# Four graph layers on one core: the last layer's sum over heads in halves and partly on TensorE, and a weight-turning stage folded into the next

## The reference

```python
# third layer, after attention: enc is [2048, 512]
out = relu(enc @ W1.T + b1)      # W1 256x512
out = relu(out @ W2.T + b2)      # W2 128x256
out = relu(out @ W3.T + b3)      # W3 256x128
out = out @ W4.T + b4            # W4 512x256
# fourth layer, 8 heads of 64, 10000 pairs (sub, obj) among the first 1500 rows
q = inst[sub] @ Wq.T + bq;  k = inst[obj] @ Wk.T + bk
scores = zeros(8, n, n).at[:, sub, obj].set((q * k).sum(-1) / 8)
scores = where(mask, -inf, scores); diagonal set to 1e-7
attn = softmax(scores, axis=2)
return (attn.sum(axis=0) / 8) @ inst
```

## Time and profile before

| | |
|---|---|
| median of 3 runs | 4013.73 us (4013.5 to 4014.74) |
| the profiled execution | 4014.29 us, span 4012.5 us |
| busy over the span | PE 3447.6 us (86%), DVE 3285.9 (82%), ACT 2812.9 (70%), POOL 1317.8 (33%) |
| mean granted clock of PE | 0.922 |
| relation stage, first `peaks` to last `finish` | 3316.42 to 4006.81 us |
| its busy times | DVE 631.3 us, PE 612.4, ACT 330.2 |

### The profile page before, as it was taken

The page is one execution under the profiler, slowest core; times in us unless marked ns, Lnnn a source line. Parts: engine busy times, 40 slices in busy tenths (PEclk is TensorE's granted clock), DMA queues, the critical chain, the costliest instruction groups (busy, mean ns, idle before and its releaser), DMA issues. The chain is left out here.

```text
span 4012.5 us, 55910 instructions
## 1 busy us (share of the span) xinstructions
PE 3447.6 (86%) x20136; PEld 2041.2 (51%) x20136; DVE 3285.9 (82%) x5486; ACT 2812.9 (70%) x3711; POOL 1317.8 (33%) x1035
## 2 busy tenths in 40 slices
PE   7899999879899744889999848999997997989898
PEld 4799999434444322444444414378775443333333
DVE  4799998579999798599999875399996408999997
ACT  5799998459899998399989971377784325444443
POOL 0476443014445355044445342056550200000000
PEclk9999999889999876999999969999998998989989
DMA  7711110311111020311111005210001211111110
GB/s 242 261 45 34 30 34 13 98 45 50 51 42 45 25 76 28 109 48 37 32 40 40 14 6 181 115 23 22 20 21 48 75 41 58 48 45 40 53 37 16
DMA packets 167767, 229.14 MB, mean 57 GB/s; under 512 B 90578, under 2 KB 101744, under 8 KB 164240
## 3 DMA queue, kind: packets, MB, share of 16 engines
q1 hardware_dynamic: 148592, 182.94, 14.5%
q0 software_dynamic: 18896, 42.46, 3.3%
HBM read 150.19 MB, written 74.89 MB: 56 GB/s over the span
## 5 line engine op out<-in xcount | busy, mean ns | idle before, releaser
L1736 DVE SCALAR_TENSOR_TENSOR junk<-expd,mid 128x2048 bf16<-128x2048 f32 x440 | 1034.8, 2352 | 14.1
L594 ACT ACTIVATE steepz<-s1b,thr_h 128x512 bf16<-128x512 f32 (+1 forms) x928 | 774.3, 916 | 32.0 <-DVE A L665 20.8
L1624 ACT ACTIVATE junk_s<-expd,nmid 128x2048 bf16<-128x2048 f32 x244 | 486.5, 1994 | 5.3 <-POOL nmid L1690 2.7
L1627 ACT ACTIVATE junk_s<-expd,nmid 128x2048 bf16<-128x2048 f32 x244 | 486.6, 1994 | 0.0
L748 PE MATMUL acc<-V,B 128*128 128x198 bf16 x4096 | 443.1, 251 | 34.2 <-DVE B L667 13.6
L755 PE MATMUL acc<-V,adjT 128*128 128x99 bf16 (+1 forms) x5248 | 417.0, 218 | 0.3 <-issue 0.3
L2217 PE MATMUL psS<-KT,qs 64*128 64x512 f32 x1024 | 333.0, 684 | 74.3 <-DVE m L2318 69.5
L1688 POOL TENSOR_SCALAR reach<-above,lack 128x1 f32<-128x1 f32 x196 | 203.2, 1037 | 579.6 <-ACT lack L1635 579.2
L1690 POOL TENSOR_SCALAR nmid<-reach,steps,nmid 128x1 f32<-128x1 f32 x196 | 357.7, 1825 | 20.6
L755 PEld LDWEIGHTS acc<-V,adjT 128*128 128x128 bf16 x5248 | 341.1, 98 | 40.6 <-issue 1.4
L748 PEld LDWEIGHTS acc<-V,B 128*128 128x128 bf16 x4096 | 342.1, 99 | 38.0 <-issue 23.8
(11 more groups left out here) (309 smaller groups left out, 6433.7 us busy)
## 6 DMA issues: line engine op xcount, KB each, us to landing
rows<-in_adj_dram SPq DMA_DIRECT2D x16, 1024.0 KB, 8.7
s1b<-sT_dram SPq DMA_DIRECT2D x32, 512.0 KB
block<-adj_dram SPq DMA_DIRECT2D x32, 512.0 KB, 4.4
plain_table<-rows POOLq DMA_DIRECT2D x16, 512.0 KB, 8.0
adj_dram<-adjT POOLq DMA_DIRECT2D x4, 2048.0 KB, 21.2
veil_table<-fill POOLq DMA_DIRECT2D x64, 128.0 KB
y_dram<-yo SPq DMA_DIRECT2D x32, 256.0 KB, 2.0
step_dram<-xo SPq DMA_DIRECT2D x32, 256.0 KB, 2.0
```

Of the source, the lines that this page charges most:

```text
L594: act.activation(steepz[:, m % RELUS, :], s1b[:, q % 4, :], ACT.Relu, bias=thr_h[:, u, 1, j:j + 1], scale=STEEP).then_inc(relu_ready, 1)
L1624: act.activation(junk_s[:, 0, :], expd[:, slot[i], :], ACT.Relu, bias=col(nmid, i), accum_out=col(above, i)).then_inc(sums_ready, 1)
L1627: act.activation(junk_s[:, 1, :], expd[:, slot[i], :], ACT.Sign, bias=col(nmid, i), accum_out=col(signs, i)).then_inc(sums_ready, 1)
L1736: link(dve.scalar_tensor_tensor(junk[:, :], e, col(mid, i), e, ALU.is_gt, ALU.mult, accum_out=found))
```

## The change

In the perceptron, `weight_transpose_stage` is gone. Its four loads stand at the head of SP's program in the real stage, and its twenty turns are packed in six units (4, 4, 2, 2, 4 and 4 blocks), one behind each of the first six tiles on PE, each with one ACT copy, through the buffer `psN` that `weights` uses too. ACT's wait for the biases moves from the head of its program to iteration 6.

In the relation layer (names as above):

- Of the eight heads, 0 to 4 go through DVE's sum. Head 5 is the buffer that they are summed into; `attn` is gone. Heads 6 and 7 are only scaled, on ACT (`scale`, 2048 columns each), and PE adds the three parts while it turns them: each block of `psT` is three accumulating turns in place of one, 48 per tile in place of 16.
- The sum on DVE is cut in halves of 1024 columns: 12 instructions per tile in place of 8 of 2048, halves in alternation, so that each needs the one before the last.
- G grows from 10 slots to 8 short-lived and 6 long-lived; `attnT` shrinks to three groups; the output row is written over the input row.
- All orders are new. An iteration has eight steps n. PE: n=0 S0 A7 (of tile t-3); n=1 S1 T0; n=2 S2 T1 A0 A1; n=3 S3 T2 A2; n=4 S4 T3 A3; n=5 S5 A4; n=6 S6 A5; n=7 S7 A6. DVE, with W a half-width sum: n=0 P0, W11 and diagonal of tile t-2, finish of t-3; n=1 P1, weights, W0, W1; n=2 to 4 P and two W; n=5 to 7 P and one W.

```diff
--- before.py
+++ after.py
...
-    def weight_transpose_stage(self, items):
...
-            def _(pe):
-                for i, (n, r, c) in enumerate(blocks):
-                    pe.wait_ge(w_in[n], 16)
-                    if i >= 4:
-                        pe.wait_ge(t_copied, i - 3)
-                    pe.transpose(psT[:, i % 4, 0:P], loads[n][:, r, tile(c)], self.ident[:, :]).then_inc(t_ready, 1)
...
-            def _(act):
-                for i, (n, r, c) in enumerate(blocks):
-                    act.wait_ge(t_ready, i + 1)
-                    act.copy(items[n][1][:, c, tile(r)], psT[:, i % 4, 0:P]).then_inc(t_copied, 1)
...
-            self.weight_transpose_stage([(a["L2_gnn_W1"], w1t), (a["L2_gnn_W2"], w2t),
-                                         (a["L2_gnn_W3"], w3t), (a["L2_gnn_W4"], w4t)])
+            raw = [self.sb(st, "raw", [P, w.shape[0] // P, w.shape[1]])
+                   for w in (a[f"L2_gnn_W{i}"] for i in (1, 2, 3, 4))]
...
+            units = [(0, [(r, k) for k in range(KD)], w1t[:, :, tile(r)]) for r in range(E1)]
+            units += [(1, [(0, c) for c in range(E1)], w2t[:, :, :]),
+                      (2, [(r, 0) for r in range(E3)], w3t[:, 0, :].rearrange("p (r i) -> p r i", r=E3))]
+            units += [(3, [(r, c) for r in range(KD)], w4t[:, c, :].rearrange("p (r i) -> p r i", r=KD)) for c in range(E3)]
...
+                for i in range(4):
+                    sp.dma_start(raw[i][:, :, :], a[f"L2_gnn_W{i + 1}"].rearrange("(r p) c -> p r c", p=P)
+                                 ).then_inc(raw_in[i], 16)
...
+                def small_weights(n):
+                    _, blocks, dst = units[n]
+                    act.wait_ge(wt_ready, n + 1)
+                    act.copy(dst, psN[:, n % 2, 0:len(blocks), :]).then_inc(wt_copied, 1)
...
-                act.wait_ge(b_in, 64)
                 for t in range(NT + 1):
                     if t < NT:
                         exps(t)
+                    if 1 <= t <= UNITS:
+                        small_weights(t - 1)
                     if t >= 9:
                         weights(t - 9)
+                    if t == 6:
+                        act.wait_ge(b_in, 64)
...
+                def small_weights(n):
+                    i, blocks, _ = units[n]
+                    pe.wait_ge(raw_in[i], 16)
+                    if n >= 2:
+                        pe.wait_ge(wt_copied, n - 1)
+                    for k, (r, c) in enumerate(blocks):
+                        mm = pe.transpose(psN[:, n % 2, k, :], raw[i][:, r, tile(c)], self.ident[:, :])
+                    mm.then_inc(wt_ready, 1)
...
                     self.transpose_tiles(pe, psT, t, nat, t_ready, t_copied)
+                    if t < UNITS:
+                        small_weights(t)
...
-        SLOTS = 10
+        SCALED = 2
+        SUM = H - SCALED - 1
+        HEADS_DONE = 2 * (SUM + 1)
+        SUMMED = HEADS_DONE + 1
+        LONG = SCALED + 1
+        SHORTS, LONGS = 8, 6
+        TURNED = 3
...
-            Gb = self.sb(st, "Gb", [P, SLOTS - H // 2, N])
...
-            attn = self.sb(st, "attn", [P, 2, N])
-            attnT = self.sb(st, "attnT", [P, NT, P])
+            attnT = self.sb(st, "attnT", [P, TURNED, 4, P])
...
-                return Ga[:, n, :] if n < H // 2 else Gb[:, n - H // 2, :]
+                return slot((t * SUM + h) % SHORTS if h < SUM else SHORTS + (t * LONG + h - SUM) % LONGS)
+
+            def parts(t):
+                return [G(t, h) for h in range(SUM, H)]
...
-                            sp.wait_ge(weighed, (H + 1) * (t - 2) + 1)
+                            sp.wait_ge(weighed, SUMMED * (t - 2) + 4)
...
-                            sp.wait_ge(xo_ready, t - 3)
+                            sp.wait_ge(x_out[t % 2], 16 * (t // 2 - 1))
...
-                        pe.wait_ge(weighed, (H + 1) * (t + 1))
+                        pe.wait_ge(weighed, SUMMED * (t + 1))
+                        pe.wait_ge(scaled, SCALED * (t + 1))
                     if t >= 1 or gp >= 1:
                         pe.wait_ge(t_copied, 4 * t + gp)
                     for j in range(4):
-                        mm = pe.transpose(psT[:, j, :], attn[:, t % 2, tile(4 * gp + j)], self.ident[:, :])
+                        for n, part in enumerate(parts(t)):
+                            mm = pe.matmul(psT[:, j, :], part[:, tile(4 * gp + j)], self.ident[:, :],
+                                           start=(n == 0), stop=(n == SCALED), is_transpose=True)
...
-                    if gp == 3 and half == 1:
+                        mm = pe.matmul(psO[:, :], attnT[:, (4 * t + gp) % TURNED, j % 4, :], nat[:, j, :], start=(j == 0), stop=(j == NT - 1))
+                    if half == 1:
                         mm.then_inc(o_ready, 1)
 
+                turned = {1: (0,), 2: (1,), 3: (2,), 4: (3,)}
+                applied = {2: (0, 1), 3: (2,), 4: (3,), 5: (4,), 6: (5,), 7: (6,)}
                 for t in range(NT + 2):
                     if t < NT:
                         pe.wait_ge(q_in[t % 2], 16 * (t // 2 + 1))
-                    for m in range(PAIRS):
+                    for n in range(2 * PAIRS):
                         if t < NT:
-                            scores(t, m, 0)
+                            scores(t, n // 2, n % 2)
+                        if n == 0 and t >= 3:
+                            apply(t - 3, 3, 1)
                         if t >= 2:
-                            transposes(t - 2, m)
-                        if t >= 2 and m >= 1:
-                            apply(t - 2, m - 1, 0)
-                        if t < NT:
-                            scores(t, m, 1)
-                        if t >= 2 and m >= 1:
-                            apply(t - 2, m - 1, 1)
-                    if t >= 2:
-                        apply(t - 2, 3, 0)
-                        apply(t - 2, 3, 1)
+                            for gp in turned.get(n, ()):
+                                transposes(t - 2, gp)
+                            for part in applied.get(n, ()):
+                                apply(t - 2, part // 2, part % 2)
+                apply(NT - 1, 3, 1)
...
-                    if t >= 1 and gp == 0:
-                        act.wait_ge(o_ready, t)
-                    act.copy(attnT[:, 4 * gp:4 * gp + 4, :], psT[:, :, :]).then_inc(t_copied, 1)
+                    if 4 * t + gp >= TURNED:
+                        act.wait_ge(o_ready, 4 * t + gp - TURNED + 1)
+                    act.copy(attnT[:, (4 * t + gp) % TURNED, :, :], psT[:, :, :]).then_inc(t_copied, 1)
...
+                def exps(t, h):
+                    act.wait_ge(scores_read, unit(t, h // 2, 1, h % 2) + 1)
...
+                def scale(t, h):
+                    act.wait_ge(r_ready, t + 1)
+                    act.activation(G(t, h), G(t, h), ACT.Copy, scale=r[:, h:h + 1]).then_inc(scaled, 1)
 
...
+                    if t >= 2:
+                        copies(t - 2, 0)
+                    if t < NT:
+                        exps(t, 0)
+                        exps(t, 1)
+                    if t >= 2:
+                        copies(t - 2, 1)
+                    if 1 <= t <= NT:
+                        scale(t - 1, SUM + 1)
+                    if t >= 2:
+                        copies(t - 2, 2)
+                    if t < NT:
+                        exps(t, 2)
+                        exps(t, 3)
+                    if t >= 2:
+                        copies(t - 2, 3)
+                    if t < NT:
+                        exps(t, 4)
+                        exps(t, 5)
+                        count(t)
+                    if 1 <= t <= NT:
+                        scale(t - 1, SUM + 2)
+                    if t < NT:
+                        exps(t, 6)
+                        exps(t, 7)
...
+                        if t * SUM + h >= SHORTS:
+                            before = t * SUM + h - SHORTS
+                            dve.wait_ge(weighed, SUMMED * (before // SUM) + 2 * order.index(before % SUM) + 2)
+                    elif t * LONG + h - SUM >= LONGS:
+                        dve.wait_ge(t_ready, 4 * ((t * LONG + h - SUM - LONGS) // LONG) + 4)
...
-                        elif t * H + h >= SLOTS:
-                            before = t * H + h - SLOTS
-                            dve.wait_ge(weighed, (H + 1) * (before // H) + before % H + 1)
+                        else:
+                            slot_free(t, h)
...
+                    if t >= 1:
+                        dve.wait_ge(scaled, SCALED * t)
...
-                    link(dve.tensor_scalar(r[:, :], rz[:, :], z[:, 0:1], None, ALU.mult))
+                    dve.tensor_scalar(r[:, :], rz[:, :], z[:, 0:1], None, ALU.mult).then_inc(r_ready, 1)
+                    dve.wait_ge(r_ready, t + 1)
...
+                order = [0, None, 1, 2, 3, 4]
+
+                def weigh(t, k):
+                    cols = slice(k % 2 * HALF, (k % 2 + 1) * HALF)
```

(38 more changed lines are left out.)

82 lines of the change are left out of this document (23 added, 59 removed).

## The result

The new kernel takes 3911.5 us (median; 3909.38 to 3916.31 in 4 runs), the kernel before on the same chip 4013.61 (4012.19 to 4014.74): ratio 0.9747, 95% interval 0.9731 to 0.9764. That is 102 us less; 3926 was forecast, with a range from 3906 to 3970. The profiled execution of the new kernel took 3916.31, 98.0 less than that of the kernel before. It divides so: 84.65 in the relation stage (first `peaks` to last `finish` 690.39, now 605.74) and 13.34 ahead of it. It is the slowest of the four, 4.8 above their median.

A forecast was written before the change was run, and what follows sets the result against it. DVE (94% busy) and PE (91%, inflated by a slow clock behind a hole) were taken to bound the relation stage. From 4014.3, less 74.7 there and 13.5 in the perceptron, came 3926.1 us, range 3906 to 3970.

The forecast's parts named there:

- a hole with a slow clock: Old relation stage, before the third call of `scores`: 3.2 us with 0.09 us of PE work, then 7.0 us at 0.51.
- DVE's prices: DVE work per relation tile: eight P, 12 half sums at 1.20, `weights`, `diagonal` and `finish`, 35.8 us in all.
- PE's prices: PE work per relation tile at full clock: 36.0 us, with 0.117 per further turn and 1.43 for T of twelve.
- The chain of one period: Relation period: PE leads from S2 to S0, 28.82, then 2.22 to P0, 4.64 to P1, 1.34 to S2; 37.0 us.
- ACT at no cost: Two scalings per relation tile, 4 us on ACT, were costed at nothing, hidden while ACT waits for DVE's minima.
- The waits of no cost: Relation period: P4's second instruction waits for T3 with no air, T0 waits for the diagonal; both cost nothing.
- The stage: Relation stage: first period -5.4, thirteen periods -65.9, last -4.9, tail +1.5 (41.5, PE doing two tiles); sum -74.7 us.
- The perceptron: Ahead of the relation stage: first exponential 15.7 us earlier, about 2 given back waiting for the first weight; 13.5 gained.
- The slow clock once per tile: Rival: in the relation stage 7.6 us per period stay slow; period 40.8, +53, 3979 us; chance 0.13.
- Accumulating turns don't overlap: Rival: each accumulating turn on PE waits for the last, 0.273 us; period 43.9, total 4038 us; chance 0.05.
- Hand-overs take more: Rival: lateness passes between level engines in the relation stage; period 38.5, +21, 3947 us; chance 0.18.
- Less than priced: Rival: period bounded below by 35.8 and perceptron gain by 15.7, 3907 us or a little less; under 3906 chance 0.03.

## Why the prediction was right

**The bound.** The prediction read the stage as two level engines and a hole with a slow clock. The sums one step later in the old kernel took away the hole and gave 31.6 us, with DVE then the wall; the new kernel with a hole ahead of S3 lost 63.6 us again. Both halves of that reading are shown, the level engines by the kernels with one head fewer off DVE and with a fourth turn.

**DVE's prices.** 35.8 per tile was priced, 35.66 measured; a half sum 1.20, measured 1.20. "Dropping two heads and halving is worth 3.7 us" was 3.75 (39.41 to 35.66), made of 4.5 for the heads (40.21 to 35.66) and 0.7 to 0.8 given back by the halves, as the full-width sums show.

The Trainium skill ("VectorE: DVE Perf Modes", the section on the TRN2 errata) has a fixed extra per instruction that small tiles pay again and again. The full-width run agrees: six instructions fewer per tile are 0.70 us of DVE's busy time, 0.117 each.

**PE's prices.** A further turn was put at 0.117, from turns at the lower clock, and called the least that it could take; it took 0.109, so that bound was wrong. T of twelve was 1.43, is 1.36, and A A behind it 3.53 and not 3.64. This is the whole of the 0.32 by which T1 to the next S0 is shorter (26.58 against 26.90).

**The chain of one period**, term by term: P1 to T1 3.26, measured 3.25 (3543.55 to 3546.80); T1 to S0 26.90, measured 26.58 (to 3573.38); S0 to P0 2.22, measured 2.11 (to 3575.49); P0 to P1 4.64, measured 4.54 (to 3580.03). Sum 37.0, measured 36.48. All four errors have one sign, and over 13 periods they are 6.7 us (481.3 forecast, 474.6 measured).

**ACT at no cost.** No wait of DVE or PE in the new kernel's twelve periods is put down to a scaling; ACT is busy 24.3 of 36.5.

**The waits of no cost.** P4's second instruction was said to have no air towards T3; it has 0.4 us, since T3's turns end at 3560.24 (3558.71 + 1.53) and the instruction starts at 3560.65. What holds P4 was not seen in the prediction: its own slot, read until just then by the half sum ahead of it, 0.23 us. With the row of plain edges third this wait is gone.

**The stage.** First period 35.6 forecast, 35.22 measured. Last 32.3, measured 31.72. Tail 41.5, measured 39.24, so 0.8 less than before and not 1.5 more: the mis-sized terms are those of PE with nothing between them, 19.93 per tile (3868.81 to 3888.74) and not 21.1: A takes 1.72 in a row of A and not 1.82, T 1.31 to 1.36 and not 1.43, and twice 1.2 is the whole of it. The end of the stage, PE with nothing between:

```profile
3868.81 1.53 PE L2237 MATMUL psT<-ident,Gb 128*128 128x128 f32 x12 [1.73 <-DVE Gb L2392]
...
3872.38 3.60 PE L2246 MATMUL psO<-B,attnT 128*128 128x512 f32 x8
3875.82 1.47 PE L2237 MATMUL psT<-ident,Gb 128*128 128x128 f32 x12
...
3888.74 1.47 PE L2237 MATMUL psT<-ident,Gb 128*128 128x128 f32 x12
```

Sum -74.7, measured -84.65; 6.7 of the 10 are the thirteen periods, 2.3 the tail, 1.0 the first and the last. So 3926.1 lies 9.8 above the profiled execution, all of it in this stage, and 14.6 above the median; the other 4.8 are how far that execution is from the median, which no term could have had.

**The perceptron.** Forecast -13.5. The exponentials gained 15.69 against the loads (15.7 was said). Given back at the first `hidden`: 0.8 and not 2.2 (it came 14.9 sooner), about as long as PE's wait of 0.79 for the first weight, though no run shows that it is that wait. One more is gone by the end of the stage, 13.9. That the total meets the forecast's 13.5 to 0.4 us is partly luck, as the same code of this stage took 222.62 to 231.49 us in other kernels.

**The rivals.** *The slow clock once per tile*: the clock stays at 1.00 through twelve periods with 48 turns each, the stretch with T0, S, T1 among them. That the clock can fall in nearly this order the hole ahead of S3 shows: there it fell behind twelve turns, the first matmuls of S3 and an idle stretch. Whether it would have fallen with other matmuls in place of those turns, no run shows.

The Trainium skill ("TensorE: Matmul & The Clock Gate", Part 4, PE-mode transpose) says that transposes don't count as PE being busy for the clock. The runs don't bear it out as something that costs here: with a fourth turn per block, 64 turns per tile, the clock is still 1.00. Nearer to a test is the end of the new kernel's stage, where 5.30 us hold nothing but idle time and 24 turns, and the clock is 1.00 in them and in the 7.62 us behind:

```profile
3867.08:3872.38 5.30, 2.89 (x24) 2.66 (x25) 4.89 (x15) 3.06 (x7) 0.54 (x1) 1.00 0.13 49
3872.38:3880.00 7.62, 7.62 (x37) 4.65 (x36) 7.62 (x7) 3.08 (x3) 0.00 (x0) 1.00 0.13 34
```

That speaks against turns counting for nothing, since the old kernel's 3.2 us of almost no PE work were enough for a fall. But the fall in the run with the hole would fit the page's rule, as turns stand ahead of the idle time there; no run was made to separate the two.

*Accumulating turns don't overlap*: 0.109 each, not 0.273. *Hand-overs take more*: the four links of the chain each took less than priced. *Less than priced* had 0.03 for a time under 3906, which did not come; in part it is what happened: 36.49 lies between the 37.0 of the chain and the 35.8 below which the period could not go.

## What to carry to other kernels

When two engines are level, work has to leave one without lengthening the other by more: here the 4.5 us that two heads cost DVE went to ACT's idle time and 3.5 us of accumulating turns on PE, and one head fewer or the turns of one more were both slower by 1.3 to 1.6 us per period. Close a long hole in an engine's work before counting that work, where its clock falls after the hole: behind 3 us of waiting per tile the next 7 us ran at 0.51 of the full clock, and moving each sum by one step took 31.6 us off the old kernel. Cutting an instruction in two has a price, here 0.70 us of DVE per tile, and needs somebody who waits for the first half; no run shows one here. With the last sum out of step 0 full width and halves differ by 0.13 us per period, so where the sums stand mattered more than how wide they are.

## What the runs showed of the hardware

Accumulating float32 turns into one place of PSUM run at 0.109 us each at clock 1.00, three deep, and four deep as well (16 in 1.80 us).

Behind an idle stretch of PE of 1.7 us the clock was 0.65 over the next 4.9 us; behind the old kernel's 3.2 us it was 0.51 over 7.0. The 0.3 us ahead of T0 cost nothing. But at the end of the stage idle stretches of 1.73 (new kernel) and 1.74 us (the run with the hole) left the clock at 1.00. They follow eight matmuls of A, where the 1.7 us follow twelve turns and the first matmuls of S3. So the length of the idle stretch alone does not tell; what does stays open.

The same code of the perceptron's stage took 222.62 to 231.49 us in the profiles of different kernels. The groups of two tiny DVE instructions in it (line, shapes, busy and mean ns), first in the new kernel, where the stage took 229.85 us:

```profile
L149 DVE SCALAR_TENSOR_TENSOR nmr<-mv,rstd 128x4 f32<-128x4 f32 x4 | 3.6, 912 | 0.1
L138 DVE TENSOR_SCALAR veps<-mv 128x4 f32<-128x4 f32 x4 | 3.5, 879 | 0.1
```

and in the one with full-width sums, where it took 223.07:

```profile
L149 DVE SCALAR_TENSOR_TENSOR nmr<-mv,rstd 128x4 f32<-128x4 f32 x4 | 2.1, 516 | 0.1
L138 DVE TENSOR_SCALAR veps<-mv 128x4 f32<-128x4 f32 x4 | 1.2, 296 | 0.1
```

In one timeline of the new kernel the same operation lasts 3.16 or 0.16 us:

```profile
3157.60 3.16 DVE L149 SCALAR_TENSOR_TENSOR nmr<-mv,rstd 128x4 f32<-128x4 f32 x1
3157.68 1.28 POOL L989 TENSOR_TENSOR xt<-xt,b 128x512 f32<-128x512 f32 x1
3159.46 1.27 POOL L989 TENSOR_TENSOR xt<-xt,b 128x512 f32<-128x512 f32 x1
...
3167.29 0.16 DVE L149 SCALAR_TENSOR_TENSOR nmr<-mv,rstd 128x4 f32<-128x4 f32 x1
```

The long one lies over two additions of POOL and ends with the second, and ACT waits for it; the long L138 (2.95 us, at 3171.46) does the same. That POOL's work on SBUF holds DVE up is what the rows suggest; the groups above account for at most 3.8 of the 6.8 us between these two kernels; the rest and what decides it from one profile to the next stay open, and no run was made to separate it.
